# A three-layer attention kernel: the first layer's attention worked chunk by chunk, with its keys streamed piece by piece

## The chip, the core and the metric

One core of a Trainium2 chip runs the whole program. The metric is the device time of one execution in microseconds (us); a change is judged by the medians of repeated runs. The engines are TensorE (PE in the rows; PEld is its weight load), VectorE (DVE), ScalarE (ACT), GpSimd (POOL) and SyncE (SP), whose queue issues every DMA of this kernel.

## What is computed

The input is 2048 tokens of 256 features. Three attention blocks stand in a row, with feed-forward and linear blocks between them, each behind a layer norm and added to its input. The change touches the first of them alone; cut to it:

```python
def _L0_attn_a_ref(x, Wq, Wk, Wv, Wo):          # H = 16 heads of 16 features
    q, k, v = ((x @ W).reshape(B, T, H, Dh) for W in (Wq, Wk, Wv))
    scores = jnp.einsum('bthd,bshd->bhts', q, k)
    mask = jnp.tril(jnp.ones((T, T), dtype=scores.dtype))
    scores = scores * mask                       # zero above the diagonal, not -inf
    attn = jax.nn.softmax(scores / T ** 0.5, axis=-1)
    out = jnp.einsum('bhts,bshd->bthd', attn, v).reshape(B, T, H * Dh)
    return out @ Wo
x = x + _L0_attn_a_ref(_layernorm(x), ...)
x = x + _L0_ffn_ref(_layernorm(x), ...)
x = x + _L0_attn_b_ref(_layernorm(x), ...)       # linear attention, a cumulative sum
x = x + _L0_ffn_ref(_layernorm(x), ...)
```

A masked score is zero, so every later key still adds exp(0 - max) times its value to a token's sum. The kernel adds these "rests" from suffix sums of the values.

## The kernel before

The 16 heads stand in 4 groups (NG) of 4 heads, the 2048 tokens in 4 chunks (NC) of 512. A **cell** is one group and one chunk of queries. Each attention (`Layer`, lines 83 to 218) has two kinds of work, which one list of steps (`Layer.steps`, written by `Layer.plan`) interleaves; every engine walks the same list in order and waits on semaphores.

The first kind finds each row's maximum. A "max" step is a pair of products of 128 queries with up to 512 keys (`max_pair`, L871), each into one of three PSUM banks, the slots (`SLOTS`), and VectorE reduces each (L1309; with the mask on the diagonal L1305). When a cell's are done, "neg" reduces over the pieces (L1318), "mtr" transposes the 16 columns on TensorE (L910), VectorE splits them in two parts (L1324, L1326), and SP sends them as extra rows of the queries with eight small DMAs (`max_rows`, L517). In the text a **block** is one such product at full width: 512 keys, one reduction. The first layer has 544 blocks.

The second kind uses them. A "score" step is a pair of products of 128 keys with the chunk's 512 queries, the extra rows subtracting the maximum (L932). ScalarE takes the exponential of the pair (L1093), GpSimd masks the diagonal (L689), and "pv" multiplies with the values (L953). In the text a **unit** is 128 keys against a full chunk for one group: two score steps, two exponentials, one pv step of four products. The first layer has 136 full units' worth. The first score of a cell waits for its rows (`max_rows_in`); "save" (L1098) and "otr" (L914, L1339 to L1344) take the result out, "shift" (L1082, L679) makes the factors of the rests.

The cells go group by group: group 0 with chunks 0 to 3, then group 1. The stacked keys and queries of a group lie in one half of KR and QR, and the next group's are loaded into the other half by `load_stacks` (L495) in twelve DMAs of 256 KB. In the projection before the attention, `project` (L476) writes the parts of q and k to DRAM, and `load_chunk` reads group 0's back, 64 KB a DMA, four of them behind each of the later three stores of a chunk. The parts pass through a ring of two tiles, STG: ScalarE writes the high part (L1039), VectorE the low part (L1167), and ScalarE may write a tile again when its store has landed (`parts_out`). `plan` spaces the max steps evenly against the units by a target line.

The rests' products (`rest_products`, L860 and L861: 62 products of 128x256) stand as one piece ahead of the first score step; their suffix sums lie in PF, where the exponentials go later, and their banks are 4 to 7.

Of the kernel before, what the change touches and what calls it, by code (L numbers as in the profile page):

```python
# [31 lines left out]
P = 128  # L32
T, D, HID = 2048, 256, 1024
H, DH = 16, 16
NB = T // P
# [25 lines left out]
SLACK = 9.0  # L61

# [12 lines left out]
def slot_of(n):  # L75

    return (n - 1) % SLOTS, (n - 1) // SLOTS + 1


def slots_to(n):  # L80

    return [(i, (n - i + SLOTS - 1) // SLOTS) for i in range(SLOTS) if n > i]


class Layer:


    def __init__(self, name, causal, zeros, rope, sem):
        self.name, self.causal, self.zeros, self.rope = name, causal, zeros, rope

        self.units, self.chunk_first, self.chunk_last = [], [], []
        for g in range(NG):
            for c in range(NC):
                self.chunk_first.append(len(self.units))
                for sb in range(BPC * (c + 1) if causal else NB):
                    self.units.append((g, c, sb, max(0, sb - BPC * c) * P if causal else 0))
                self.chunk_last.append(len(self.units) - 1)
# [4 lines left out]
        for g in range(NG):  # L102
            for tb in range(NB):
# [8 lines left out]
        self.plan()  # L112
        s = lambda x: sem(f"{name}_{x}")
        self.stack_in = s("stack_in")
        self.ones_in = s("ones_in")
        self.max_rows_in = s("max_rows_in")
        self.rope_in = s("rope_in")
        self.slot_ready = s("slot_ready")
# [13 lines left out]

    def diagonal(self, u):
        _, c, sb, off = self.units[u]
        return self.causal and sb >= BPC * c

# [81 lines left out]
TAKES = {"max": 2, "mtr": 1, "otr": 1, "rope": 1}  # L218


def build(nc, a, out):
# [3 lines left out]
    with ctx:  # L225
# [56 lines left out]
        SEL = sb("SEL", [P, 2])  # L282
        PS = ctx.enter_context(nc.psum_tensor("PS", [P, 8 * CH], F32))
# [14 lines left out]
        FS = PF[:, 0:(NB - 1) * D].rearrange("p (b d) -> p b d", d=D)  # L298
        TRI = PF[:, (NB - 1) * D:(NB - 1) * D + P]
        ONES = PF[:, (NB - 1) * D + P:NB * D]  # L300
# [33 lines left out]
        L0 = Layer("a", True, True, False, sem)  # L334
        L1 = Layer("b", False, False, False, sem)
        L2 = Layer("c", True, False, True, sem)
# [33 lines left out]
        x_done = sem("x_done")  # L370
        ar_made = sem("ar_made")
# [8 lines left out]
        def wave(*kinds):  # L380

            return [(kinds[i], c) for t in range(2 * len(kinds) + NC) for i in range(len(kinds)) for c in [t - 2 * i] if 0 <= c < NC]
# [61 lines left out]
        def _(sp):  # L444
# [79 lines left out]
            def attention_steps(L):  # L524
# [4 lines left out]
                for g in range(1, NG):  # L529
                    for i in range(3):  # L530
                        stacks[max(0, (g - 1) * L.n_group - 1) + STACK_STEP * i] = (g, i)
# [892 lines left out]
```

## Time and profile before

| | |
|---|---|
| median of 3 runs | 2735.32 us (2732.45 to 2740.95) |
| the profiled execution | 2741.86 us, its span 2740.1 us |
| TensorE busy | 2499.6 us (91%), granted clock 0.92 of full on average |
| VectorE busy | 1884.0 us (69%) |
| ScalarE busy | 1231.1 us (45%) |
| first layer's attention | about 83 to 608 us of the span |

The rows are read as follows. Times count from the span's start. The clock column (PEclk) is 1.00 for TensorE's upper level, 2.4 GHz, and 0.50 for its lower level, 1.2 GHz. A busy time is the union of the instructions' spans. In an idle bracket stands what ended the wait. A row of busy times by stretch has, after the stretch and its length, the busy us of PE, PEld, DVE, ACT and POOL, each with its count of instructions, then the granted clock, the DMA engines' busy share and GB/s.

### The profile page before, as it was taken

Reading aid. Unit: us, or ns where it says so; the run is one execution under the profiler, and the core shown is the slowest. Engines: PE = TensorE matmul, PEld = TensorE weight load, DVE = VectorE, ACT = ScalarE, POOL = GpSimd, SP = SyncE. Lnnn points to the kernel's source line nnn. Section 1 sums busy time; section 2 is a strip of 40 time slices with the busy share of each in tenths; the row PEclk is TensorE's granted clock in tenths of the full one; section 3 lists DMA queues with packets and bytes.
Section 4 is the critical chain, followed back from the end, with each engine's and each line's share of the span. In section 5 each row is a group of like instructions: output and inputs, shape, how many; then the busy total and the mean of one; then the engine's idle time right before and its main releaser. Section 6 shows DMA issues by size and latency. Waiting matters only on the chain. (4 is left out here: it accounts for less than half of the span.)

```text
span 2740.1 us, 38483 instructions
## 1 busy us (share of the span) xinstructions
PE 2499.6 (91%) x13878; PEld 1264.1 (46%) x13878; DVE 1884.0 (69%) x4855; ACT 1231.1 (45%) x1494; POOL 149.0 (5%) x330
## 2 busy tenths in 40 slices
PE   6999999989999997999999999988779999999985
PEld 4544333335565554433333333334436556555644
DVE  5577888836345532889898988873847877776618
ACT  3234566761111112167676767665121345555540
POOL 2200111110000000000000000000000001010100
PEclk9756999999999998599999999999876999999998
DMA  6330312000000005210300300000173426262200
GB/s 201 90 40 2 47 17 32 1 20 1 1 1 0 12 1 173 31 16 1 47 1 1 47 1 2 1 1 16 39 205 94 99 80 112 70 111 70 55 1 31
DMA packets 68147, 121.51 MB, mean 44 GB/s; under 512 B 11890, under 2 KB 29554, under 8 KB 64370
## 3 DMA queue, kind: packets, MB, share of 16 engines
q1 hardware_dynamic: 67956, 119.06, 19.5%
q8 instruction: 109, 1.79, 0.3%
q14 instruction: 82, 0.67, 0.1%
HBM read 79.92 MB, written 38.27 MB: 43 GB/s over the span
## 5 line engine op out<-in xcount | busy, mean ns | idle before, releaser
L1093 ACT ACTIVATE PF<-PS 128x1024 f32<-128x1024 f32 (+3 forms) x1152 | 1053.6, 953 | 819.2 <-PE PS L932 491.5
L1309 DVE TENSOR_REDUCE MP<-PS 128x1 f32<-128x512 f32 x1408 | 877.8, 682 | 161.2 <-PE PS L871 156.0
L871 PE MATMUL PS<-KR,QR 48*128 48x512 f32 (+3 forms) x2304 | 784.4, 482 | 87.3 <-DVE MP L1309 34.8
L871 PEld LDWEIGHTS PS<-KR,QR 48*128 48x128 f32 x2304 | 357.5, 203 | 638.7 <-DVE MP L1309 325.8
L953 PE MATMUL PS<-PF,VO 128*32 128x512 f32 (+3 forms) x4608 | 606.6, 601 | 0.2
L932 PE MATMUL PS<-QR,KR 50*128 50x512 f32 (+3 forms) x2304 | 512.4, 431 | 25.9 <-DMA QR<-MRL 17.9
L1305 DVE CUSTOM_DVE_ANT_0 JUNK<-PS,WA 128x512 bf16<-128x512 f32 (+3 forms) x512 | 286.9, 605 | 102.1 <-PE PS L871 52.7
L932 PEld LDWEIGHTS PS<-QR,KR 50*128 50x128 f32 x2304 | 250.5, 197 | 212.6 <-ACT PF L1093 140.1
L741 PE MATMUL PS<-RQ,RK 64*128 64x512 f32 (+3 forms) x1920 | 274.5, 371 | 0.0
L735 PE MATMUL PS<-HT,WA 128*128 128x512 f32 x512 | 221.1, 592 | 0.0
L689 POOL TENSOR_SCALAR_AFFINE_SELECT PF<-PF 128x256 f32<-128x256 f32 x256 | 103.9, 409 | 2104.0 <-ACT PF L1093 2100.6
L741 PEld LDWEIGHTS PS<-RQ,RK 64*128 64x128 f32 x1920 | 195.5, 191 | 25.0
L953 PEld LDWEIGHTS PS<-PF,VO 128*32 128x32 f32 x4608 | 93.0, 110 | 163.1 <-issue 124.4
L735 PEld LDWEIGHTS PS<-HT,WA 128*128 128x128 f32 x512 | 96.6, 190 | 118.6 <-issue 115.7
L996 ACT COPY HT<-PS 128x512 f32<-128x512 f32 x64 | 34.5, 588 | 225.1 <-PE PS L769 225.1
L1305 DVE CUSTOM_DVE_ANT_0 JUNK<-PS,MASK 128x128 bf16<-128x128 f32 (+3 forms) x256 | 113.1, 487 | 25.8 <-PE PS L871 24.5
L1156 DVE TENSOR_TENSOR X<-PS,X 128x512 f32<-128x512 f32 x48 | 33.1, 690 | 134.9 <-PE PS L839 99.5
L1059 ACT ACTIVATE PF<-PS 128x512 f32<-128x512 f32 x64 | 38.2, 598 | 167.4 <-PE PS L735 167.4
L839 PE MATMUL PS<-WA,QF 128*128 128x256 f32 x512 | 111.8, 379 | 0.0
L839 PEld LDWEIGHTS PS<-WA,QF 128*128 128x128 f32 x512 | 97.3, 190 | 16.6 <-issue 3.8
L735 PE MATMUL PS<-HT,WB 128*128 128x512 f32 x224 | 100.3, 603 | 0.0
L1202 DVE SCALAR_TENSOR_TENSOR PF<-PF,PS 128x512 f32<-128x512 f32 x64 | 43.9, 685 | 74.3 <-ACT PF L1059 74.3
(139 smaller groups left out, 1434.1 us busy)
## 6 DMA issues: line engine op xcount, KB each, us to landing
WA<-rope_scores SPq DMA_DIRECT2D x66, 256.0 KB, 3.2
rope_scores<-WA SPq DMA_DIRECT2D x22, 256.0 KB, 2.7
QR<-parts_a_q SPq DMA_DIRECT2D x18, 256.0 KB, 6.1
KR<-parts_a_k SPq DMA_DIRECT2D x18, 256.0 KB, 9.5
QR<-parts_b_q SPq DMA_DIRECT2D x18, 256.0 KB, 11.3
KR<-parts_b_k SPq DMA_DIRECT2D x18, 256.0 KB, 14.6
QR<-parts_c_q SPq DMA_DIRECT2D x18, 256.0 KB, 6.5
KR<-parts_c_k SPq DMA_DIRECT2D x18, 256.0 KB, 9.4
```

The costliest lines, as they stand in the source:

```text
L689: g_.affine_select(out=tile, in_=tile, compare_op=ALU.is_ge, fill=0.0, base=0, pattern=[[0, 2], [1, P]], channel_multiplier=-1).then_inc(L ...
L735: ins = mm(dst, left(k), right(k), start=k == 0, stop=k == n - 1)
L741: return mm(dst, left[rows, i, l0:l0 + m], right[rows, k, r0:r0 + n], start=start and r == 0, stop=r == len(ROPE_PARTS) - 1)
L839: ins = mm(bank(b, D, i * D), GT[:, m, blk(2 * h + i)], WDT[:, m, :], start=m == 0, stop=m == HID // P - 1)
L871: mm(bank(slots[h][0], w), QR[rows, t0 + tb * P:t0 + (tb + 1) * P], KR[rows, t0 + s0:t0 + s0 + w], start=True, stop=True).then_inc(L.slot_ ...
L932: ins = mm(dst[h], KR[rows, t0 + sb_ * P:t0 + (sb_ + 1) * P], QR[rows, t0 + c * CH + off:t0 + (c + 1) * CH], start=True, stop=not L.rope)
L953: ins = mm(PS[32 * j:32 * j + 2 * DH, 7 * CH + off:8 * CH], v_tile(sb_, HG * g + j), PT[:, u % SETS, j, off:CH], start=first, stop=last, t ...
L1059: sc.activation(TH[:, n % 2, :], bank((d0 + 2 * m) % 4), ACT.Tanh, scale=0.5).then_inc(tanh_ready, 1)
L1093: sc.activation(PT[:, u % SETS, 2 * q:2 * q + 2, off:CH], src, ACT.Exp).then_inc(L.exp_done, 1)
L1202: v.scalar_tensor_tensor(out=TA[:, n % 2, :], in0=TH[:, n % 2, :], scalar=1.0, in1=bank(bg), op0=ALU.add, op1=ALU.mult).then_inc(d_free, 1)
L1305: ins = v.tensor_tensor_reduce(out=JUNK[:, h * CH:h * CH + w], in0=src, in1=other, scale=1.0, scalar=LOWEST, op0=ALU.add, op1=ALU.max, acc ...
L1309: ins = v.reduce_max(MP[:, i, c, y:y + 1], src, AX.X)
```

## The change

Only the first layer's attention is reordered (`by_chunk`); the other two keep `plan`, and the order of what follows the first attention stays as it was. The change has five parts.

- The cells go chunk by chunk: chunk 0 for the four groups, then chunk 1, up to chunk 3. `plan_by_chunk` writes the steps. A max step is placed only when the target asks for it and, by the planner's own clock, its keys are in place (`in_place`, `LOAD_TIME`).
- Keys are streamed. `plan_batches` makes 40 batches, one for each cell and 512-key piece: six DMAs of 64 KB for the keys and, with piece 0, six more for the queries. A batch is issued when the scores that last read its place are done (`load_batch`). Queries lie in a ring of four cells.
- The four batches of chunk 0 are issued inside the projection of chunk 1, twelve DMAs behind each of its four stores. The loads behind the stores of chunks 2 and 3, and those at the head of the attention, are gone.
- The rests' products go through the three slots, one step for each of eight results, spread among the max steps of cell 1, and their suffix sums lie in QF's upper half.
- Steps for work of the next blocks under the attention (`fill_steps`, `under`) are there, but `FILLED = 0`: none is placed.

```diff
+FILLED = 0
+Q_CELLS = 4
+IN_RING = 4
+LOAD_TIME = 12.0
...
+        self.cells = [(g, c) for c in range(NC) for g in range(NG)] if by_chunk else [(g, c) for g in range(NG) for c in range(NC)]
...
+    def q_col(self, g, c, p):
+        if self.by_chunk:
+            return (self.cell_of(g, c) % Q_CELLS * NP + p) * CH
+        return (g % 2 * NP + p) * T + c * CH
+
+    def k_col(self, g, c, p):
+        if self.by_chunk:
+            cell = self.cell_of(g, c)
+            return (cell % 2 * NP + p) * T + (2 * CH * (cell // 2 % 2) if c < 2 else 0)
+        return (g % 2 * NP + p) * T
+
+    def plan_batches(self):
+
+        self.batches, reader = [], {}
+        after = -1
+        for cell, (g, c) in enumerate(self.cells):
+            k0 = self.k_col(g, c, 0)
+            for i in range(c + 1):
+                after = max(after, reader.get((k0 // CH) + i, -1))
+                if i == 0 and cell >= Q_CELLS:
+                    after = max(after, self.chunk_last[cell - Q_CELLS])
+                self.batches.append((cell, i, after))
+            for i in range(c + 1):
+                reader[(k0 // CH) + i] = self.chunk_first[cell] + BPC * (i + 1) - 1
...
+        for cell in range(len(self.cells)):
+            first = cell_jobs[cell][1:] if cell else cell_jobs[0]
+            ones += [max_step(n) for n in first]
+            if cell == 1:
+                rests = [(0.0, 1.75, ("rest", n)) for n in range(NB // 2 - 1, -1, -1)]
+                mine = ones[-len(first):]
+                del ones[-len(first):]
+                while mine or rests:
+                    ones += rests[:1] + mine[:2]
+                    rests, mine = rests[1:], mine[2:]
+            ones.append((0.35, 0.0, ("neg", cell)))
+            if cell + 1 < len(self.cells):
+                ones.append(max_step(cell_jobs[cell + 1][0]))
+            ones.append((0.8, 0.15, ("mtr", cell)))
...
+        def in_place():
+            if ones[at][2][0] != "max":
+                return True
+            g, _, tb, i = self.jobs[ones[at][2][1]][:4]
+            n = self.batch_no[self.cell_of(g, tb // BPC), i]
+            return n in loaded and loaded[n] <= clock
+
+        for cost, step in twos:
+            if step[0] == "score" and step[1] in self.chunk_first and step[2] == 0:
+                cell = self.chunk_first.index(step[1])
+                while at <= max(at_step["mtr", cell], at_step["rest", 0]):
+                    give()
+                steps.append(("shift", cell))
+            room = 1.3
+            while at < len(ones) and given < target(run + cost / 2) and room > 0.1 and in_place():
+                room -= ones[at][0]
+                give()
...
+            steps.append(step)
+            run += cost
+            clock += cost
+            if step[0] == "score" and step[2] == NP - 1:
+                for n, (_, _, after) in enumerate(self.batches):
+                    if after == step[1]:
+                        loaded[n] = clock + LOAD_TIME
...
-                    if c > 0:
+                    if L.by_chunk and c == 1:
+                        load_batch(L, i)
+                    if c > 0 and not L.by_chunk:
                         load_chunk(L, c - 1, range(3 * i // len(tiles), 3 * (i + 1) // len(tiles)))
...
+            def load_batch(L, n):
+
+                cell, i, _ = L.batches[n]
+                g, c = L.cells[cell]
+                if n >= IN_RING:
+                    sp.wait_ge(L.batch_in[n % IN_RING], L.batch_count[n - IN_RING])
+                    settled("sp", sp)
...
+                for m in range(3):
+                    for h in range(2):
+                        rows = slice(HALF * h + m * DH, HALF * h + (m + 1) * DH)
+                        if i == 0:
...
+                            sp.dma_start(dst, src[h]).then_inc(L.batch_in[n % IN_RING], 16)
...
+                        sp.dma_start(dst, src[h]).then_inc(L.batch_in[n % IN_RING], 16)
...
+                    if L.by_chunk and step[0] == "score" and step[2] == NP - 1:
+                        due = [n for n, (_, _, after) in enumerate(L.batches) if after == step[1]]
+                        if due:
+                            sp.wait_ge(L.score_ready, 2 * NP * (step[1] + 1))
+                            settled("sp", sp)
+                        for n in due:
+                            load_batch(L, n)
```

How the order moves, at three places. First comes SyncE's queue in the projection of chunk 1 (PF is STG's memory, L476 a store, L495 a load; now L683, and L723 and L726). Before:

```order
L476 DMA parts_a_q<-PF 128x2x512 x2
L495 DMA QR<-parts_a_q 16x2x512 x2
L495 DMA KR<-parts_a_k 16x2x512 x2
L476 DMA parts_a_k<-PF 128x2x512
L495 DMA QR<-parts_a_q 16x2x512 x2
L495 DMA KR<-parts_a_k 16x2x512 x2
L476 DMA parts_a_k<-PF 128x2x512
L495 DMA QR<-parts_a_q 16x2x512 x2
L495 DMA KR<-parts_a_k 16x2x512 x2
```

and now:

```order
L683 DMA parts_a_q<-PF 128x2x512
L723 DMA QR<-parts_a_q 16x2x512
L726 DMA KR<-parts_a_k 16x2x512
L723 DMA QR<-parts_a_q 16x2x512
L726 DMA KR<-parts_a_k 16x2x512
L723 DMA QR<-parts_a_q 16x2x512
L726 DMA KR<-parts_a_k 16x2x512
L723 DMA QR<-parts_a_q 16x2x512
L726 DMA KR<-parts_a_k 16x2x512
L723 DMA QR<-parts_a_q 16x2x512
L726 DMA KR<-parts_a_k 16x2x512
L723 DMA QR<-parts_a_q 16x2x512
```

Between two stores of chunk 1 stood four loads at most. Now twelve stand behind each of its four stores: of those behind the second, ten are shown and one more of each kind follows before the third store.

Second comes TensorE's queue where the maxima of a cell of chunk 2 are turned (L910 before, L1221 now; L871 and L1116 are max steps, L932 and L1241 scores, L953 and L1262 pv). Before, for cell 7:

```order
L953 MATMUL PS<-PF,VO 32x512 x4
L871 MATMUL PS<-KR,QR 128x512 x2
L932 MATMUL PS<-QR,KR 128x512 x4
L871 MATMUL PS<-KR,QR 128x128 x2
L910 MATMUL PS<-IDF,MX 16x128
L953 MATMUL PS<-PF,VO 32x512 x4
L871 MATMUL PS<-KR,QR 128x128 x2
L871 MATMUL PS<-KR,QR 128x256 x2
L932 MATMUL PS<-QR,KR 128x512 x4
```

and now, for cell 8, the first of chunk 2:

```order
L1221 MATMUL PS<-IDF,MX 16x128
L1116 MATMUL PS<-KR,QR 128x512 x2
L1241 MATMUL PS<-QR,KR 128x512 x2
L1116 MATMUL PS<-KR,QR 128x512 x2
L1241 MATMUL PS<-QR,KR 128x512 x2
L1116 MATMUL PS<-KR,QR 128x512 x2
L1262 MATMUL PS<-PF,VO 32x256 x4
```

Before, that cell's own scores follow later, 25 steps of the list behind its transpose; now the cell's first score, the second row behind the transpose, has one max step ahead of it.

Third comes TensorE's queue behind the transpose of cell 9, now:

```order
L1221 MATMUL PS<-IDF,MX 16x128
L1241 MATMUL PS<-QR,KR 128x512 x4
L1116 MATMUL PS<-KR,QR 128x512 x2
L1262 MATMUL PS<-PF,VO 32x512 x4
L1241 MATMUL PS<-QR,KR 128x512 x4
L1262 MATMUL PS<-PF,VO 32x512 x4
L1241 MATMUL PS<-QR,KR 128x384 x4
L1262 MATMUL PS<-PF,VO 32x512 x4
L1241 MATMUL PS<-QR,KR 128x256 x4
L1262 MATMUL PS<-PF,VO 32x512 x4
L1241 MATMUL PS<-QR,KR 128x128 x4
L1262 MATMUL PS<-PF,VO 32x384 x4
```

Scores and pv steps stand here with one max step among them, where before one stood between nearly every two rows.

## Rows read from the trace of the kernel before

**Rows 1.** The page of the profile: busy time, share of the span, instructions.

```profile
PE 2499.6 (91%) x13878; PEld 1264.1 (46%) x13878; DVE 1884.0 (69%) x4855; ACT 1231.1 (45%) x1494; POOL 149.0 (5%) x330
```

**Rows 2.** Busy time by stretch, the first layer's attention: stretch, then each engine's, clock, DMA.

```profile
103.90:120.90 17.00, 16.23 (x65) 13.53 (x64) 0.84 (x4) 4.82 (x9) 0.00 (x0) 0.85 0.00 0
255.00:564.50 309.50, 287.53 (x1864) 119.48 (x1861) 263.92 (x678) 197.95 (x254) 46.56 (x117) 0.96 0.17 22
325.30:352.90 27.60, 25.16 (x164) 10.44 (x163) 24.23 (x74) 17.26 (x23) 2.46 (x7) 1.00 0.01 1
358.90:397.20 38.30, 36.07 (x223) 14.84 (x222) 34.27 (x92) 25.12 (x30) 2.45 (x6) 1.00 0.01 2
582.00:602.00 20.00, 18.67 (x124) 5.30 (x122) 1.13 (x4) 18.45 (x20) 1.50 (x4) 1.00 0.00 1
```

**Rows 3.** Busy time by stretch, those with a lowered clock.

```profile
126.00:258.00 132.00, 128.37 (x513) 55.33 (x514) 93.79 (x247) 50.31 (x63) 10.80 (x27) 0.53 0.20 25
297.00:321.00 24.00, 21.61 (x118) 8.90 (x118) 17.87 (x44) 11.99 (x17) 4.43 (x11) 0.79 0.71 88
412.00:424.00 12.00, 11.15 (x44) 4.84 (x44) 7.73 (x22) 6.16 (x8) 0.37 (x1) 0.57 0.99 129
571.50:581.50 10.00, 9.94 (x51) 3.20 (x52) 0.00 (x0) 7.79 (x9) 0.00 (x0) 0.57 0.01 2
```

**Rows 4.** Timeline of the projection: start us, us, engine, line, operation [idle before].

```profile
53.75 2.06 SPq L476 DMA_DIRECT2D parts_a_q<-PF  x2
55.86 1.30 SPq L495 DMA_DIRECT2D QR<-parts_a_q  x2
57.21 0.89 SPq L495 DMA_DIRECT2D KR<-parts_a_k  x2
...
67.73 0.60 ACT L1039 ACTIVATE PF<-PS 128x512 fp32r<-128x512 f32 x1 [1.96 <-DMA parts_a_q<-PF]
...
79.77 0.69 DVE L1167 SCALAR_TENSOR_TENSOR PF<-PS,PF 128x512 fp32r<-128x512 f32 x1 [2.30 <-ACT PF L1039]
...
82.32 0.59 ACT L996 COPY VO<-PS 128x512 f32<-128x512 f32 x1 [0.77 <-PE PS L735]
```

**Rows 5.** Timeline of the head: first max product, first transpose, first score.

```profile
83.00 0.41 PE L871 MATMUL PS<-KR,QR 48*128 48x128 f32 x3 [0.72 <-issue]
...
92.26 0.37 PE L910 MATMUL PS<-IDF,MX 128*16 128x128 f32 x1 [0.23 <-DVE MX L1318]
...
120.87 0.50 PE L932 MATMUL PS<-QR,KR 50*128 50x512 f32 x2 [0.77 <-ACT WB L996]
```

**Rows 6.** Timeline of ScalarE: the "shift" of cell 3 and of cell 15.

```profile
233.87 0.23 ACT L1082 ACTIVATE EM<-MX 128x16 f32<-128x16 f32 x1
...
564.44 0.23 ACT L1082 ACTIVATE EM<-MX 128x16 f32<-128x16 f32 x1
```

**Rows 7.** Timeline of a unit's pv at either clock level, TensorE.

```profile
243.86 1.93 PE L953 MATMUL PS<-PF,VO 128*32 128x512 f32 x8
...
259.02 1.07 PE L953 MATMUL PS<-PF,VO 128*32 128x512 f32 x8
```

**Rows 8.** Timeline of cell 15's rows, from transpose to first score.

```profile
564.49 0.27 PE L910 MATMUL PS<-IDF,MX 128*16 128x128 f32 x1 [0.55 <-DVE MX L1318]
...
565.48 2.42 SPq L517 DMA_DIRECT2D QR<-MRH  x4
...
567.94 2.42 SPq L517 DMA_DIRECT2D QR<-MRL  x4
...
571.44 1.22 PE L932 MATMUL PS<-QR,KR 50*128 50x512 f32 x4 [5.90 <-DMA QR<-MRL]
```

**Rows 9.** DMA issues of the whole run: KB each, us from issue to landing.

```profile
KR<-parts_a_k SPq DMA_DIRECT2D x18, 256.0 KB, 9.5
QR<-parts_a_q SPq DMA_DIRECT2D x24, 64.0 KB, 3.5
KR<-parts_a_k SPq DMA_DIRECT2D x24, 64.0 KB, 3.0
```

More of the change, by code:

```diff
@@ L131, in __init__, with cell_of, place @@
         self.chain = s("chain")
+    def cell_of(self, g, c):
+        return self.cells.index((g, c))
+    def q_col(self, g, c, p):
[19 more added lines that the diff above has]
+                reader[(k0 // CH) + i] = self.chunk_first[cell] + BPC * (i + 1) - 1
+        self.batch_no = {(cell, i): n for n, (cell, i, _) in enumerate(self.batches)}
+        self.batch_count, done = [], [0] * IN_RING
+        for n, (cell, i, _) in enumerate(self.batches):
+            done[n % IN_RING] += 16 * 6 * (2 if i == 0 else 1)
+            self.batch_count.append(done[n % IN_RING])
+    def place(self):
+        uses, order, held = [0] * SLOTS, list(range(SLOTS)), None
+        self.slot_at, self.taken = {}, []
+        for step in self.steps:
+            slots = []
+            if step[0] == "fd" and step[4] > 0:
+                if step[4] == 3:
+                    held = None
+            else:
+                for _ in range(TAKES.get(step[0], 0)):
+                    slot = next(x for x in order if x != held)
+                    order.remove(slot)
+                    order.append(slot)
+                    uses[slot] += 1
+                    slots.append((slot, uses[slot]))
+            if step[0] == "fd" and step[4] == 0:
+                held = slots[0][0]
+            assert not slots or step not in self.slot_at
+            if slots:
+                self.slot_at[step] = slots
+            self.taken.append([(x, n) for x, n in enumerate(uses) if n])
     def diagonal(self, u):
@@ L673, in attention_steps @@
                         cell = step[1]
-                        g, c = divmod(cell, NC)
+                        g, c = L.cells[cell]
+                        x = cell % 2
+                        for half in range(2):
+                            slot, uses = L.slot_at["rest", 2 * c + half][0]
+                            pool.wait_ge(L.slot_free[slot], uses)
                         pool.wait_ge(L.shift_exp, cell + 1)
@@ L1152, in residual @@
+            c_under = Count()
             def residual(c):
```

498 lines of the change are left out of this document (380 added, 118 removed).

## The prediction

> **What bounds the kernel now.** I read the page first: TensorE is busy 91% of the span, VectorE 69% [rows 1]. Then the stretches of the first layer's attention, since the order of all that follows it is unchanged. At the full clock, 255 to 564.5 us, TensorE is busy 93% and VectorE 85% [rows 2]: two engines near their limits, and the even mixture of max steps and units is what keeps both busy. A stretch without disturbance is 358.9 to 397.2 us: by the list of steps it holds 12.5 units and 53 blocks, so 0.72 us a block, with TensorE busy 94% and VectorE 89% [rows 2]. The tail has no max steps: ScalarE is busy 92% there and does 20 exponentials in 20 us [rows 2], so a unit takes 2.0 us. Early on the clock is low: 126 to 258 us at 0.53, TensorE busy 97% [rows 3]; a unit's four pv products take 1.93 us there against 1.07 [rows 7]. So early TensorE is the bound alone, later the mixture is.
>
> I compare the two orders by place: so many units and blocks done. Before, the shift of cell 3 runs at 233.9 us, with 19.5 units and 150 blocks placed; that of cell 15 at 564.4 us, with 121.5 units and all 544 blocks [rows 6]. From there on the two orders are alike (14.5 units and the end).
>
> **The change part by part.**
>
> *Projection.* The stores of chunk 1 begin at 53.75 us; four loads behind one take 1.30 + 0.89 = 2.2 us of SP's queue [rows 4]. Twelve take 6.6 us. New chain: stores of chunk 1 at 54, 61, 68 and 75, the last batch ends at 82. ScalarE may refill a STG tile when its store has landed, so chunk 2's first two tiles go out at 82, the next two 2.8 us (landing) + 0.6 + 0.7 later at about 86, chunk 3's first two at 90 to 91, its last two pass ScalarE at 94 to 95, and the last copy of values ends at about 96. Before, that copy ended at 82.9 [rows 4] and the first max product began at 83.0 [rows 5]. **+13 us**, between 5 (the queue catches up, since later chunks carry no loads) and 16.
>
> *Head.* Before, 37.9 us passed from the first max product to the first score [rows 5], of which the rests alone took 17 with VectorE idle [rows 2]. Now cell 0 takes the same 9.6 us to its transpose [rows 5], then the rests' 17 us carry seven max steps between them, 10 blocks, whose products cost TensorE some 3 us more: 29.6 us. First score at 96 + 30 = 125.6: **+5 us** in all, with 20 blocks done where before 28 were.
>
> *Early cells, low clock.* Before, 113 us took the program from the first score to 19.5 units and 122 further blocks. The comparable place of the new order, 146 blocks, has 24.5 units: five units and four blocks more. At half the clock a unit costs TensorE 1.93 us for pv and four score products of 0.43, 3.7 us together; 5 x 3.7 + 4 x 0.43 = **+20 us**. Bounds: 5 x 2.0 = 10 at the full clock, 30 if the short cells 0 to 3 wait for their rows as well.
>
> *Evenness.* `in_place` withholds max steps while keys load, and both rules of `room` and target then crowd them. In the list six stretches, beginning at 24.5, 43, 57.5, 67.5, 91 and 107.5 units, hold 42.5 units and only 24.5 blocks. VectorE has nothing to do there and units go at the tail's pace: 42.5 x 2.0 = 85 us. The other 373.5 blocks of this part go at VectorE's pace. Its busy time was 263.9 us for some 380 blocks at the full clock [rows 2], 0.69 a block; it can't be all busy, and 0.72 was reached in an even stretch. I take 0.74, between 0.69 and the 0.79 of 325.3 to 352.9 us, where narrower pieces make up part of 35 blocks [rows 2]: 276 us. Together 361 us where before 330.5 passed [rows 6]: **+31 us**, bounds +12 and +50.
>
> *Waits for the rows.* From cell 15's transpose to its first score took 6.95 us, 5.9 of them idle [rows 8]: two VectorE instructions, eight DMAs of 0.6 us in SP's queue, a landing. Before, only cell 15 had so little work in between. Now cells 8 and 12 have one max step (1.3 us) there, cells 10 and 11 three max steps (3.4 us), and cell 13 has work enough but six loads ahead of its rows in SP's queue (2.7 us). 2 x 5.6 + 2 x 3.5 + 2.7 = **+21 us**. What queues behind the waiting score is everything, max steps too, so VectorE idles with it. Bounds 8 and 30.
>
> *Clock behind those waits.* Behind the one wait of before, the clock was at 0.57 for 10 us [rows 3]. Four of the five waits lead into a stretch of scores and pv, where such 10 us do 2.7 units and not 5: about +16. Against it, the two lowered stretches at group starts before, 297 to 321 and 412 to 424 us [rows 3], cost some 30% of 36 us, and there are no group starts now: -11. **+5 us**.
>
> *Loads.* 336 loads of 64 KB take the place of 48 such and 36 of 256 KB. Six issue in 2.7 us and land 3.0 us later [rows 4, 9]; the tightest later piece has some 8 us in the list. Nothing, as long as 64 KB lands so fast. The placement of the rests' sums, the semaphore for each slot and GpSimd's two more waits cost nothing: each is met long before.
>
> Sum: 5 + 20 + 31 + 21 + 5 = 82; I take **+80 us**. Against the profiled execution's 2741.9 us that is 2822; the median is 6.5 us below that execution, so 2815. About 8 us either way (0.3%) is what a measurement of this kernel can tell from no change.
>
> TensorE was busy 97% of 126 to 258 us and its clock stayed at the lower level for nearly all of it [rows 3]. The Trainium skill ("TensorE: Matmul & The Clock Gate", Part 1: The HAM clock gate) says the opposite: the throttled state is the default and activity releases it. By row the sum is +82, by that rule the early part would run at the full clock and the sum would be +45. The trace does not agree with the rule there.
>
> **The rivals.**
>
> *Order doesn't matter* (15%). TensorE is the bound at 94% and its total is conserved, so crowded and empty stretches balance. Then evenness and its clock term cost nothing: 80 - 36 = +44, 2779. Against it: ScalarE bound the tail, and 0.69 us a block is VectorE's own time.
>
> *Full clock early* (13%). The short cells and the dense rests' products hold the clock up. Then 126 blocks at 0.76 take 96 us and not 133: -37, 2778. The rule named above says so; the row speaks against it.
>
> *Low clock late* (14%). Waits and empty stretches pull the clock down again and again. At half the clock the empty stretches cost 42.5 x 3.7 = 157 us and the crowded ones, by TensorE, 54.5 x 3.7 + 373.5 x 0.43 = 362: +158 if all were so, +50 for a third: 2865.
>
> *Late keys* (5%). If the small loads land as slowly as those of 256 KB, 9.5 us [rows 9], ten tight pieces are 3 to 4 us late each: +35, 2850. The Trainium skill ("DMA: Bandwidth & Descriptors", Bandwidth) wants transfers of 1 MiB and calls those under 64 KB descriptor-dominated; our row has them land sooner, not later.
>
> *Faster, by the clock alone* (4%). Before, the lowered stretches held 132 us that did 137 blocks, worth 104 us at 0.76, and 36 us at 30%: 28 + 11 = 39 us to gain if none of it returns. The early term falls to 10. That wins only if the rest, projection, evenness and waits, stays under 29: with evenness and the projection at nothing and waits at 21, less 8 for the rests beside maxima, it is 39 - 23 = -16: 2719.
>
> *Nothing measurable* (3%): terms at their low bounds with a better clock.
>
> **How the numbers follow.** The forecast as summed has 46%. The range 2765 to 2868 takes in the low bounds of projection, evenness and waits, the two rivals at 2779 and most of the low clock; outside are the last two cases and the worst of the low clock, under two in ten. Faster 0.04, same 0.04, slower 0.92, from the same cases.
>
> **What the new profile would show.** The first max product near 96 us, with ScalarE's L1039 rows waiting on stores for 4 us and more. The first score near 126. Waits of 3 to 6 us of the score row on the rows' DMAs at cells 8, 10, 11 and 12. Stretches of some 12 to 19 us in which VectorE is under 30% busy and ScalarE over 90%. The last block near 645 us, the attention's end near 688. Stages behind it as long as before. If the first max product stands at 85, the projection step is wrong; if VectorE's idle time doesn't sit in those stretches, evenness is.

## The result, and the profile after

The changed kernel takes 2887.3 us (median of 4 runs, 2881.1 to 2890.4), the kernel before on the same chip 2738.1 us: 1.054 times as long, 95% interval 1.0508 to 1.0573, some 149 us slower. The forecast was 2815, the range ended at 2868. The direction was right, the size was not. The profiled execution took 2890.4 us, its span is 2888.6; that of before had 2740.1.

Where do 148.5 us of span come from? The program is cut at two points, the first and the last "shift" of layer A (ScalarE's EM rows; those of cells 3 and 15 before are [rows 6]). In the views of busy time by stretch, the columns are stretch, length, busy us of PE, PEld, DVE, ACT, POOL, then clock, DMA share, GB/s. Before:

```profile
120.62:564.44 443.82, 417.39 (x2374) 175.72 (x2374) 359.30 (x927) 249.72 (x318) 59.33 (x148) 0.83 0.18 23
564.44:2740.00 2175.56, 1991.15 (x11177) 1027.71 (x11177) 1460.23 (x3733) 949.35 (x1120) 59.13 (x148) 0.94 0.19 42
```

After:

```profile
125.35:714.47 589.12, 545.14 (x2385) 219.57 (x2389) 363.59 (x932) 253.62 (x319) 59.07 (x149) 0.63 0.14 33
714.47:2888.00 2173.53, 1987.65 (x11176) 1025.29 (x11172) 1460.93 (x3733) 948.42 (x1120) 58.98 (x148) 0.94 0.19 42
```

The first shift comes 4.7 us later, the part from first to last takes 145.3 us more, and all behind it 1.5 us less. VectorE and ScalarE are as long busy as before, within 5 us. TensorE does the same work and is busy 128 us longer, and idle 17.6 us longer (44.0 for 26.4). The busy time grew because its clock is 0.63 of full where it was 0.83. The clock has two levels, 1.2 and 2.4 GHz, so a mean of 0.63 over 589.1 us says that 2 x 0.37 x 589.1 = 436 us ran at the lower; before, 2 x 0.17 x 443.8 = 151 us. (The rounding of the mean leaves some 6 us either way.) At the lower level each microsecond does half the work: 285 us more of them cost 142. **Length less half of the low time** is 368 us before and 371 after. So within a few microseconds the length follows the clock. The measure counts an idle microsecond at the lower level for half as well, so it can't tell work from waits there. The 128 us of busy time are the clock's alone; the 17.6 us of idle time are about what the new waits for rows below come to.

The projection and the head came as forecast. ScalarE's timeline after, the copies L1347 waiting for stores [rows 4 have L1039]:

```profile
64.11 0.60 ACT L1347 ACTIVATE PF<-PS 128x512 fp32r<-128x512 f32 x1 [7.40 <-DMA parts_a_q<-PF]
...
71.52 0.60 ACT L1347 ACTIVATE PF<-PS 128x512 fp32r<-128x512 f32 x1 [4.87 <-DMA parts_a_k<-PF]
76.39 0.60 ACT L1347 ACTIVATE PF<-PS 128x512 fp32r<-128x512 f32 x1 [4.27 <-DMA parts_a_k<-PF]
82.33 0.60 ACT L1347 ACTIVATE PF<-PS 128x512 fp32r<-128x512 f32 x1 [5.35 <-DMA parts_a_q<-PF]
```

and TensorE's, its first max product and first score [rows 5]:

```profile
93.86 0.41 PE L1116 MATMUL PS<-KR,QR 48*128 48x128 f32 x3 [1.37 <-DVE PF L1565]
...
125.71 0.50 PE L1241 MATMUL PS<-QR,KR 50*128 50x512 f32 x2
```

The waits of the score row for the rows' DMAs, in the same timeline; before, cell 15 alone had one, 5.90 us [rows 8]:

```profile
322.62 0.80 PE L1241 MATMUL PS<-QR,KR 50*128 50x512 f32 x2 [5.74 <-DMA QR<-MRL]
...
418.85 1.22 PE L1241 MATMUL PS<-QR,KR 50*128 50x512 f32 x4 [2.48 <-DMA QR<-MRL]
...
469.27 1.22 PE L1241 MATMUL PS<-QR,KR 50*128 50x512 f32 x4 [2.49 <-DMA QR<-MRL]
...
530.68 0.79 PE L1241 MATMUL PS<-QR,KR 50*128 50x512 f32 x2 [5.74 <-DMA QR<-MRL]
...
595.43 0.73 PE L1241 MATMUL PS<-QR,KR 50*128 50x512 f32 x4 [0.27 <-DMA QR<-MRL]
```

These are cells 8, 10, 11, 12 and 13, 16.7 us in sum. The loads of 64 KB land in 2.6 us [rows 9 have 3.0]; no max product waited for keys.

What was not forecast shows when the middle part is cut into short stretches (busy time by stretch, after):

```profile
270.00:280.00 10.00, 8.87 (x72) 3.27 (x68) 1.30 (x5) 8.34 (x14) 3.96 (x10) 1.00 0.43 127
280.00:310.00 30.00, 27.95 (x115) 11.76 (x113) 19.79 (x51) 11.29 (x15) 2.85 (x7) 0.64 0.08 25
310.00:360.00 50.00, 42.71 (x152) 17.93 (x151) 33.45 (x84) 15.09 (x17) 1.20 (x3) 0.50 0.06 17
360.00:372.00 12.00, 11.04 (x91) 3.75 (x87) 1.85 (x4) 9.93 (x14) 3.97 (x10) 1.00 0.19 48
372.00:400.00 28.00, 25.71 (x128) 9.56 (x124) 18.00 (x48) 15.12 (x17) 0.81 (x2) 0.83 0.19 52
...
430.00:440.00 10.00, 8.76 (x53) 3.50 (x50) 7.64 (x24) 5.82 (x6) 0.00 (x0) 1.00 0.25 64
440.00:450.00 10.00, 9.89 (x39) 3.84 (x38) 7.45 (x20) 3.98 (x4) 0.81 (x2) 0.60 0.15 39
...
610.00:655.00 45.00, 44.35 (x163) 17.74 (x163) 32.27 (x69) 16.83 (x18) 1.75 (x5) 0.55 0.06 18
```

In the empty stretches, 270 to 280 and 360 to 372 us (VectorE busy 13 to 15%), the clock is full. In the crowded ones it goes to the lower level and stays: 310 to 360 at 0.50 (TensorE busy 85%, and 5.7 us of the rest are the wait at 322.62), 610 to 655 at 0.55 with TensorE busy 99%. There TensorE is the bound, not VectorE, which is busy 67 to 72%. The groups of 610 to 655 us after, max products of full width and reductions (count, busy us, mean ns, idle before):

```profile
L1116 PE MATMUL PS<-KR,QR 48*128 48x512 f32 x46 | 24.3, 725 | 0.3 <-DVE MP L1711 0.2
L1711 DVE TENSOR_REDUCE MP<-PS 128x1 f32<-128x512 f32 x42 | 26.0, 682 | 11.3 <-PE PS L1116 11.3
```

and of the even stretch before, 358.9 to 397.2 us, seen whole in [rows 2]:

```profile
L1309 DVE TENSOR_REDUCE MP<-PS 128x1 f32<-128x512 f32 x37 | 23.2, 681 | 2.4 <-PE PS L871 2.3
L871 PE MATMUL PS<-KR,QR 48*128 48x512 f32 x41 | 14.9, 473 | 1.2 <-DVE MP L1309 0.6 <-DVE MP L1305 0.2
```

A reduction takes 0.68 us in both. A full-width max product takes 0.73 us against 0.47, and VectorE, which stood idle 2.4 us before its reductions, now stands 11.3 us for them.

### The profile page after: what moved, and what is told of

It reads as the page before. It is cut to its first block, busy times and chain, and to the rows that moved or that the text cites. A ratio compares the mean times of both kernels' runs of the same rounds, so it can differ in the third digit from the quotient of the medians.

```text
span 2888.6 us, 38844 instructions
## 1 busy us (share of the span) xinstructions
PE 2619.0 (91%) x13878; PEld 1300.7 (45%) x13878; DVE 1885.6 (65%) x4855; ACT 1233.9 (43%) x1494; POOL 148.5 (5%) x330
## 4 chain that ended last, share of the span: by engine, by line
PE 57%; DVE 15%; issue 3%; ACT 2%; SPq 2%; DMA 2%; DVEq 0%; POOL 0%; ACTq 0%; POOLq 0%
PE PS L1262 15%; PE PS L1116 13%; PE PS L980 11%; DVE MP L1711 8%; PE PS L986 7%; PE PS L1241 6%; PE PS L1084 4%; ACT PF L1400 2%; DVE ST L1467 1%; SPq L704 1%; SPq L748 1%; DVE QF L1476 1%; DVE JUNK L1707 0%; DMA parts_c_k<-PF 0%; PE PS L1225 0%
## 5 line engine op out<-in xcount | busy, mean ns | idle before, releaser
L1116 PE MATMUL PS<-KR,QR 48*128 48x512 f32 (+3 forms) x2304 | 832.9, 513 | 88.5 <-DVE MP L1711 34.3
L1116 PEld LDWEIGHTS PS<-KR,QR 48*128 48x128 f32 x2304 | 379.9, 213 | 683.7 <-DVE MP L1711 334.0
L1262 PE MATMUL PS<-PF,VO 128*32 128x512 f32 (+3 forms) x4608 | 647.5, 639 | 0.1
L1241 PE MATMUL PS<-QR,KR 50*128 50x512 f32 (+3 forms) x2304 | 554.1, 453 | 47.3 <-DMA QR<-MRL 34.3
L1241 PEld LDWEIGHTS PS<-QR,KR 50*128 50x128 f32 x2304 | 266.4, 208 | 250.8 <-ACT PF L1400 168.6
L1262 PEld LDWEIGHTS PS<-PF,VO 128*32 128x32 f32 x4608 | 95.4, 113 | 175.1 <-issue 134.0
```

The lines of the kernel that those rows point to most:

```text
L1116: mm(bank(slot, w), QR[rows, q0:q0 + P], KR[rows, k0:k0 + w], start=True, stop=True).then_inc(L.slot_ready[slot], 1)
L1241: ins = mm(dst[h], KR[rows, k0:k0 + P], QR[rows, q0 + off:q0 + CH], start=True, stop=not L.rope)
L1262: ins = mm(PS[32 * j:32 * j + 2 * DH, 7 * CH + off:8 * CH], v_tile(sb_, HG * g + j), PT[:, u % SETS, j, off:CH], start=first, stop=last, t ...
```

## The experiments

Twelve kernels ran, the first four on one chip beside each other, then four, three and one. Those that start from the changed kernel ask which part of it costs; those that start from the order before make one suspected cost alone. Each is compared by ratio with the kernel before on its own chip, whose median was between 2737 and 2749 us; figures of first to last shift come from one profiled execution each.

**Piece by piece.** The changed kernel, with a cell's max steps sorted by the piece of keys, so that the last piece is asked for last.

```diff
-            for tb in range(BPC * c, BPC * (c + 1)):
+            order = [(tb, i) for tb in range(BPC * c, BPC * (c + 1)) for i in range(c + 1 if causal else NC)]
+            if by_chunk:
+                order.sort(key=lambda x: x[1])
+            for tb, i in order:
...
```

> One edit in the changed kernel: a cell's max steps are ordered by 512-key piece first and by query tile second, so that a cell's first piece can be worked on while its later pieces load. The list of steps then has no empty stretches and hardly any crowded ones: blocks in a stretch of 3 units vary by 5.4 about 12.5 instead of 8.7, and between transpose and first score every cell but the last has 7 us of work or more. If crowding is the cause (whether through the clock or by VectorE's idle time alone), the attention from cell 8 on loses most of 402 us against the even order's 300: 2790 to 2830 us. If the chunk-by-chunk order or the streaming itself is the cause, the time stays within 20 us of 2887.

Measured: 2782.6 us, 1.0102 times before (1.0037 to 1.0166), better than my theory had it. First to last shift:

```profile
127.01:599.36 472.35, 448.13 (x2380) 183.87 (x2381) 363.29 (x931) 253.63 (x318) 59.89 (x148) 0.79 0.16 41
```

117 us shorter than in the changed kernel, the low time 198 us and not 436, and length less half of it 373. The same streaming of the same pieces in the same order of cells, so most of the 149 us (105 by the medians, some 120 by the two ratios) come from the order of products within a cell. It takes two things away at once, though: most of the crowding, and all five new waits for rows, which came to 17 us.

**No load time in the plan.** `LOAD_TIME` 12.0 made 0.0, so the planner withholds nothing for a load that is under way.

> LOAD_TIME 12 becomes 0: max steps are placed as soon as their batch has been asked for. TensorE then waits for the keys themselves. The list is nearly even (4.3 about 12.5 blocks in 3 units). If crowding matters more than waits for keys: 2800 to 2850 us, with new waits of 3 to 6 us of the max row on the keys' DMAs, some ten of them. If waits for keys cost what the planner feared, it is 2887 or more.

Measured: 2883.2 us, 1.0482 (1.0426 to 1.0537), near the second of the two cases. The list is far less crowded, but the keys are then really waited for. TensorE's waits from 126 to 695 us (sum, times, longest), and first to last shift:

```profile
PE PS L1116 <- DMA KR<-parts_a_k: 61.0, 12, 9.0
```

```profile
126.42:694.82 568.40, 489.70 (x2380) 202.62 (x2381) 365.96 (x931) 253.51 (x319) 59.23 (x149) 0.69 0.13 34
```

Length less half of the low time is 392 us, the one case well over the rest: 61 us of waits stand in it, and 352 us at the lower level beside them. So here waits for keys and the lowered clock beside them cost as much as the crowding that avoids them; how much each of the two costs was not separated.

**Loads of chunk 0 spread.** Four DMAs of a batch after each store of chunks 1 to 3, the last batch at the head of the attention, in place of twelve DMAs behind each store of chunk 1.

```diff
-                    if L.by_chunk and c == 1:
-                        load_batch(L, i)
+                    if L.by_chunk and c > 0:
+                        load_batch(L, c - 1, range(3 * i // 4, 3 * (i + 1) // 4))
...
+                    load_batch(L, NG - 1)
```

> The four batches of chunk 0 are issued as the loads before were: four DMAs behind a store, one batch in each of chunks 1 to 3 and the last at the attention's head. The first max product comes at 84 to 86 us instead of 93.9. Projection term as predicted: 8 to 11 us off 2887. If the early part is bound by something behind it, less than 4.

Measured: 2877.0 us, 1.046 (1.0399 to 1.052); that interval overlaps the one of the changed kernel, so the times alone don't show the gain. The trace does. The first max product of TensorE's timeline is here at

```profile
82.30 0.41 PE L1117 MATMUL PS<-KR,QR 48*128 48x128 f32 x3 [0.72 <-DVE PF L1566]
```

11.6 us sooner than 93.86, somewhat more than expected. The first shift stands at 115.3 and not 125.4, 10.1 us sooner, and the part from first to last shift takes about as long as in the changed kernel (587.2 us). That is the price of the projection step: 10 us of the 149.

**More work for TensorE.** An extra product of 128 rows ahead of each full-width max product from cell 6 on; its output is overwritten by the max product that follows.

```diff
+                    if L.by_chunk and w == CH and L.cell_of(g, tb // BPC) >= 6:
+                        mm(bank(slot, w), KR[:, k0:k0 + P], KR[:, k0:k0 + w], start=True, stop=True)
```

> From cell 6 on a product of all 128 rows is added ahead of every full-width max product, into the same slot, and overwritten: more work for TensorE, none for any other engine, the order unchanged. If the lower clock in the crowded stretches is the cause, this holds it up there: granted clock from cell 8 to cell 15 over 0.85 instead of 0.64 and 30 to 60 us less than 2887. If the clock is only a by-product, the added products (some 370 of 0.21 to 0.43 us) make it 60 to 130 us slower, at the same clock.

Measured: 3246.0 us, 1.1767 (1.1674 to 1.186): a miss for both numbers. Groups from 130 to 1075 us, and first to last shift:

```profile
L1117 PE MATMUL PS<-KR 128*128 128x512 f32 x392 | 291.9, 745 | 0.0
```

```profile
130.60:1075.17 944.57, 918.42 (x2777) 347.98 (x2781) 391.86 (x932) 255.09 (x319) 59.08 (x148) 0.58 0.08 21
```

TensorE was busy 97% of the time and the clock sank further, 793 us at the lower level. More work in the same crowded places does not lift the clock here. Length less half of the low time is 548 us, 177 over the changed kernel's; 392 products at 0.45 us make 177, about what a full-width max product takes in the even stretch before (0.47).

**Both edits.** Piece by piece and spread loads together.

> The changed kernel with two edits at once: the maximum products of a cell run piece of keys by piece (all four row blocks against piece 0, then against piece 1, ...), and the loads for chunk 0 are issued four after each store of chunks 1 to 3 and the last ones behind the stores, not all twelve before the first store. Alone they gave -105 us (2782.6) and -10 us (2877.0). My theory (crowding of the products in the stream and the late first chunk are separate costs): 2770 to 2776, first shift about 115, first to last shift about 472 us. Rival (with the early products sooner, the stream waits for the same keys, and the second edit is worth nothing beside the first): 2780 to 2785.

Measured: 2763.3 us (10 runs), 1.0091 (1.0053 to 1.0128), some 7 to 13 us under what was expected, with 157 us at the lower level and 382 less half of it. By ratio it can't be told from piece by piece alone (1.0102), so the times leave open whether the second edit adds to the first; the first shift does come 9.9 us sooner (117.1 and 127.0). The profiled execution was the fastest of the ten, 15 us under their median:

```profile
117.12:577.54 460.42, 434.82 (x2380) 178.64 (x2381) 362.83 (x931) 253.34 (x318) 59.81 (x148) 0.83 0.16 43
```

**Both edits, 6 us reckoned for a load.** `LOAD_TIME` 12.0 made 6.0 besides.

> As the kernel with both edits, and the planner reckons 6 us for a load, not 12, so that a cell's products may be given sooner and the list becomes evener (deviation of blocks per three units 3.8, against 5.4). Theory (what is left of the loss is unevenness, and the clock that goes with it): 2755 to 2768. Rival (the planner's 12 us cover a real wait: with 6 the TensorE meets keys that are not there, as with 0): waits on keys come back, 10 us or more in sum, and the time is 2770 to 2800.

Measured: 2763.9 us, 1.0102 (1.0036 to 1.0167): inside the expected range, but no change from the kernel before it, although its list is evener. Waits for keys came to 6.3 us, under the rival's 10:

```profile
116.33:582.77 466.44, 440.12 (x2380) 184.64 (x2381) 364.86 (x931) 252.81 (x319) 59.45 (x149) 0.78 0.15 42
```

**Crowding alone.** The decisive one: the kernel before, its order of groups, its loads and its long leads, and only the planner's target made to move in steps, with one max step between two others. No max step comes later than before; half come a unit or more sooner. `held` keeps a group's products back until eleven units into the group before, when its keys are in.

```diff
-            while at < len(ones) and given < target(run + cost / 2):
+            late_on = self.zeros and step[1] >= 28
+            room = 1.3 if late_on else 1e9
+            want = -(-(run + cost / 2) // 20.5) * 20.5 if late_on else run + cost / 2
+            while at < len(ones) and given < target(min(want, whole)) and room > 0.1 and not held(step[1]):
+                room -= ones[at][0]
...
```

> The kernel before with one thing changed: from unit 28 of layer A on, the planner gives the maximum products in bunches (it aims at the next multiple of 20.5 of its own us of scores and value products, one maximum step between two of them, none of a group before its keys are in). No streaming, the old order of groups, the same loads, leads of 13 us and more before the shifts but the last. The unevenness of its list is 9.1 blocks per three units, that of the changed kernel 8.7, of before 2.8. Theory (crowding alone costs: full-clock empty stretches on the way, half clock where the products stand close, TensorE the bound there): 60 to 110 us over before, 2800 to 2855, granted clock from first to last shift about .65 to .7. Rival (the new order of cells, streaming and its waits make the loss, crowding only goes with them): within 20 us of before, 2735 to 2765, clock .8 or more.

Measured: 2874.3 us, 1.0491 (1.0443 to 1.0539), +132 over its own before, 19 us over the upper end. First to last shift, and stretches in it:

```profile
118.17:694.73 576.56, 546.37 (x2383) 221.13 (x2383) 358.39 (x929) 255.19 (x319) 59.20 (x148) 0.63 0.14 18
```

```profile
370.00:400.00 30.00, 28.83 (x110) 11.78 (x109) 20.91 (x63) 8.49 (x12) 4.01 (x10) 0.50 0.01 2
400.00:410.00 10.00, 9.71 (x52) 2.91 (x52) 1.28 (x4) 8.02 (x9) 0.00 (x0) 0.68 0.01 2
410.00:420.00 10.00, 8.16 (x44) 3.45 (x44) 8.51 (x25) 5.14 (x7) 0.00 (x0) 1.00 0.01 2
420.00:440.00 20.00, 19.84 (x67) 7.88 (x67) 13.87 (x34) 7.05 (x7) 0.00 (x0) 0.50 0.01 2
```

The clock of 0.63 and the pattern of the changed kernel are there, with nothing streamed, no new wait for a row and no new order of cells. The same products at the same count, only closer together, lose 132 us.

**The rests alone.** The order before (the changed kernel with `by_chunk` off), with the eight products of the rests set singly among the first max steps and sent through the maximum slots. Their operands stayed in PF, where the kernel before has them, and not in QF as the expectation has it.

> Of the change only the third part: the eight products of the rests go through the maximum slots, set singly among the first maximum steps behind the first transpose, and their operands stand in QF; order of groups, loads and planner as before the change. Theory (the burst of eight products that VectorE and ScalarE empty in a block holds up the stream before the first score for a few us): 0 to 8 us faster than before, first shift 113 to 121. Rival (the burst was hidden; single rests take slots from maximum products): 0 to 5 us slower.

Measured: 2743.5 us (10 runs), 0.9997 (0.9963 to 1.0031). The first shift is at 116.3 us and not 120.6, but neither that nor the rival shows in the time. This part of the change costs nothing beyond the 10 us either way that the runs leave open.

**Half, double and a fifth.** The crowding kernel with multiples of 10.25, of 41 and, after their result, of 4.1.

> The kernel before with the products bunched as in the run that had multiples of 20.5, but with multiples of 10.25, so bunches and gaps are half as long (list unevenness 5.1 blocks per three units, against 9.1 there and 2.8 before). Theory (the loss is the time that the clock spends at its lower level, half of each such microsecond, and how long the products stand close together sets that): first to last shift is about 368 us plus half the time at the lower level; some 20 to 60 us over before, 2762 to 2805, clock about .75 to .8 there. Rival (any bunching costs as much, since mean demand is the same and the clock falls at every bunch): 100 us and more over before, as with 20.5 (+132).

> The same with multiples of 41: as many products in half as many bunches, each twice as long (list unevenness 9.2, as with 20.5). Theory (the time at the lower level counts, and in long bunches at half clock TensorE is the bound): again first to last shift is 368 us plus half of the lower-level time, 560 to 600 us, clock .6 to .65, 2860 to 2900. Rival (each fall and each return of the clock has a price): with half as many of both, at least 40 us less than the 2874 of the 20.5 run.

Measured: 2856.5 us, 1.0405 (1.0359 to 1.0451), and 2868.0 us, 1.044 (1.039 to 1.049). First to last shift of each:

```profile
120.01:687.14 567.13, 537.13 (x2383) 217.80 (x2383) 358.23 (x929) 255.91 (x319) 59.47 (x148) 0.64 0.14 18
```

```profile
120.97:701.13 580.16, 550.21 (x2383) 225.24 (x2383) 358.60 (x929) 254.86 (x319) 59.69 (x148) 0.63 0.14 17
```

Half as long bunches did not halve the loss, which my theory had said; the rival held there. Twice as long bunches cost about the same, not the rival's 40 us less. The clock did not fall half as often for it, though: between the shifts the traces have 10 falls with 41 and 13 with 20.5. A price for each fall is spoken against by all the crowded kernels together: the 18 falls with 10.25 cost no more than those 13, and the 19 with 4.1 (below) least of all. What the theory had wrong was the measure, unevenness by three units. In the lists I counted instead the blocks that stand in units with four and a half blocks or more, one unit at a time: 398 and 464 here, 438 with 20.5, 435 in the changed kernel, 292 piece by piece, 218 before. That measure was then put to a test by bunches so short that the unevenness by three units is as before:

> The kernel before with the products bunched at multiples of 4.1 of the planner's us, some two units of scores and value products: by stretches of three units its list is as even as before (3.1 against 2.8), but unit by unit it is not (328 blocks stand in units with four and a half blocks or more, against 218 before, 292 in the version piece by piece, 398 with multiples of 10.25 and 435 in the changed kernel). Theory now (what lets the clock fall is how many products stand one between every two steps of the stream, even for a unit or two): 300 us or so at the lower level, 2790 to 2830. Rival (bunches as short as one unit are evened out by the slots and buffers, only those of several units count): within 15 us of before.

Measured: 2818.4 us, 1.0283 (1.0215 to 1.0351), 294 us at the lower level; both as expected of the new measure, which had been chosen after the two results above:

```profile
120.33:645.61 525.28, 492.61 (x2383) 196.26 (x2383) 359.27 (x929) 253.96 (x319) 59.45 (x149) 0.72 0.15 19
```

Eighty microseconds for max steps that stand at most two units sooner than in the kernel before, half of them a quarter of a unit or less.

**A shorter lead.** The version with both edits and 6 us a load, and a lead of 4.0 in layer A's plan for `SLACK`, which makes its list the evenest of the streamed ones (235 blocks in full units).

> The changed kernel with piece by piece products, spread chunk-0 loads and 6 us reckoned for a load, and the planner of layer A aims at a lead of 4.0 of its us, not 9.0 (list unevenness 3.3 against 3.8; most gaps between a cell's transpose and its first score shrink to some 4 us). Theory of the clock (evener is better): 2745 to 2760. Rival (the leads of 4 us are too short for the row stores and loads, so the waits for rows grow to 2 us and more at half the cells, and the clock falls behind them): 2765 to 2790.

Measured: 2750.4 us (10 runs), 1.0032 (0.9997 to 1.0068). First to last shift, and the waits for rows from 110 to 600 us:

```profile
114.50:579.34 464.84, 435.68 (x2381) 183.93 (x2379) 365.17 (x931) 251.74 (x318) 58.97 (x148) 0.79 0.16 42
```

```profile
PE PS L1245 <- DMA QR<-MRL: 13.6, 5, 5.9
```

The streamed order can thus be had for a loss that these runs can't tell from none (0.3%, some 9 us, with an interval that just reaches 1), though not for a gain over the kernel before. No version here gives one. The rival's waits for rows did come back, five of them, but not their price.

All of it in one table, from the profiled executions but for the last column:

| kernel | blocks in full units | first to last shift | low | length less half of low | ratio to before |
|---|---|---|---|---|---|
| before | 218 | 443.8 | 151 | 368 | 1 |
| shorter lead | 235 | 464.8 | 195 | 367 | 1.003 |
| both, 6 us | 259 | 466.4 | 205 | 364 | 1.010 |
| both | 292 | 460.4 | 157 | 382 | 1.009 |
| piece by piece | 292 | 472.4 | 198 | 373 | 1.010 |
| crowded, 4.1 | 328 | 525.3 | 294 | 378 | 1.028 |
| crowded, 10.25 | 398 | 567.1 | 408 | 363 | 1.041 |
| changed | 435 | 589.1 | 436 | 371 | 1.054 |
| crowded, 20.5 | 438 | 576.6 | 427 | 363 | 1.049 |
| crowded, 41 | 464 | 580.2 | 429 | 366 | 1.044 |

The length less half of the low time stays within 363 to 382 us while the length itself goes from 444 to 589. The low time rises with the blocks in full units, but not strictly (292 gives 157 and 198), and it levels off from some 400 on. Part of the scatter is that of single executions: the profiled ones of both and of piece by piece were 15 and 13 us under their medians, that of 4.1 was 11 us over. Not in the table, but off the line, is the kernel with no load time in its plan: 288 blocks, yet 352 us low, behind waits for keys.

## Why the prediction was wrong, point by point

- *Projection and head*: "First score at 96 + 30 = 125.6". Right. 93.9 and 125.7; the first score comes 4.8 us later, for +5. It is a cost of 10.9 us (83.0 to 93.9, for +13) less 6.0 gained in the head; with the loads spread the cost goes away.
- *Early cells, low clock*, +20: right. All 640 score products are in the trace, so the list's places can be found in it by counting. The changed kernel has 24.5 units and 146 blocks behind it at 263.3 us, 137.6 after its first score, where 113 passed before: +24.6. Some 122 of the 137.6 us were at the lower level.
- *Evenness*: **the step that failed** is "The other 373.5 blocks of this part go at VectorE's pace". It carried 0.74 us a block over from an even mixture at the full clock to a crowded one. The runs show that such a mixture doesn't keep that clock: at the lower level TensorE is the bound (99% busy, VectorE 72%). From 263.3 us to the last shift 451.2 us passed. Counted a little more narrowly than in the prediction, the six empty stretches hold 39.5 units and 16 blocks of it and took 95.7 us, and the waits for rows in the crowded rest 16.4. That leaves 339 us for 382 blocks: 0.89 us a block where 0.74 was forecast, 56 of the 68 us that the sum fell short. Of the crowded rest, waits included, 284 of 355 us were at the lower level. The prediction had the price for it: a crowded part all at half clock costs 362 us by its terms, not 276.
- *Its pace in empty stretches*, 2.0 us a unit, rested on ScalarE's 92% busy [rows 2]. Measured, ScalarE is busy 83% in 270 to 280 and 360 to 372 us, and the six stretches took 2.4 us a unit. Two that had the full clock throughout took 2.3 (590.6 to 606.7 us, 7 units; 658.0 to 670.4, 5.5), so the pace was somewhat too fast even without the clock.
- *Waits for the rows*, +21: right. 5.74, 2.48, 2.49, 5.74 and 0.27 us at cells 8, 10, 11, 12 and 13 against 5.6, 3.5, 3.5, 5.6 and 2.7; 16.7 in sum.
- *Clock behind those waits*, +5: right as far as it went. The empty stretches were at the lower level for 30.6 of their 95.7 us, three of them at their start and one at 373.7 to 380.5 us, which is worth 15 us against the 16 forecast. But most of it was carried in from the crowded stretches ahead, and the long low stretches are those.
- *Loads*, nothing: right as to landing. But the planner's 12 us for a load, with the order of products within a cell, are what makes the crowds, and with 0 TensorE waits 61 us for keys.
- *The rests*, the slots' semaphores: nothing, as said, within the 10 us that the run with the rests alone can tell.
- *The rivals.* "Low clock late" named the lowered clock and gave it 14%, but at "a third" of its price, with waits and empty stretches as what pulls it down; the crowding kernel has the same clock without new waits. "Order doesn't matter" was right in what it said of the work: TensorE's work is conserved, and crowded and empty stretches do balance, as the constant 363 to 382 us show. What it left out is that the clock at which the work is done isn't. No case joined the two, and so none reached 2887. "Full clock early" did not come (122 of 137.6 us low), nor did "Late keys" (no wait for them). Of the +158 that the prediction priced "if all were so", 68 us or 43% would have given the measured sum, not a third.

The range was too short for one reason: the low clock of 126 to 258 us in the trace before [rows 3] was read as a matter of the early cells. It is a crowded part too. By the list it has 122 blocks in 19.5 units, over six to a unit, where the even part has some four, and TensorE's 97% busy at half clock there is the pattern that the change spreads over layer A. (No run here thinned that early part, so that its crowding lowers the clock is an inference.) The row that would have given the price was in the prediction, and was used for the early cells alone.

## What to carry to other kernels

Where two kinds of work share TensorE and one of them is paced by another engine, the mixture has to be even from step to step, not on average: a planner that withholds work for a while and then lets it catch up at one step between every two pays in TensorE's clock, not in the waits that it shows. Split such a trace by the granted clock first, and take half of the time at the lower level off; if what is left is the same in both kernels and the engine's idle time has hardly grown, look for what lets the clock fall and not for lost overlap. And when loads gate a consumer, ask for the pieces in the order in which they arrive: here that alone gave back over 100 of 149 us, the new waits for rows among them.

## What the hardware showed that was not expected

The clock fell with TensorE 84 to 90% busy (over the 7 us before each of the changed kernel's twelve falls between the shifts) and then often stayed down with it busier than that. What it did before it fell: at the full clock the crowded steps leave it waiting for slots, as 430 to 440 us after (busy 88%) and 410 to 420 us of the crowding kernel show (82%, VectorE 85%, 1.0 of the 1.8 idle us waiting for VectorE's reductions); the next stretch is at 0.60 and 0.50. The even stretch of before, at 94% [rows 2], kept its clock. Once the clock was down, TensorE was 96 to 99% busy at the lower level for 20 to 45 us. It rose again with TensorE just as busy, often where scores and pv stand alone, and in the kernel before where the early crowd ends, at some 250 us [rows 3]. The changed kernel ahead of the rise at 428 us, with TensorE 99% busy and no max product:

```profile
420.00:428.00 8.00, 7.94 (x42) 2.44 (x44) 0.00 (x0) 6.59 (x8) 0.00 (x0) 0.50 0.09 29
```

The Trainium skill ("TensorE: Matmul & The Clock Gate", Part 1: The HAM clock gate) has activity release the throttle, and idle time bring it back. The falls agree with it, as far as the few idle microseconds before them show, and so do the rises out of busy scores and pv. But being busy was not enough: 97% busy with 392 added products of 128 rows left 793 of 944.6 us at the lower level.

What it is in the max products that keeps the clock down (their 48 rows, their small groups, the slots' waits) stays open. The runs changed their place and added others, and none changed their form.
